# Masked attention scores: VectorE adds the mask inside the maximum for 128 of 384 score units, under a re-searched order

## What is computed

```python
def _attention(v_in, k_in, q_in, mask, Wv, Wk, Wq, Wo, bo):      # L0: "self", then "cross"
    energy = jnp.einsum('nqhd,nkhd->nhqk', q, k)
    energy = jnp.where(mask == 0, jnp.float32(-1e+20), energy)
    attn = jax.nn.softmax(energy / jnp.sqrt(jnp.float32(E)), axis=-1)
    out = jnp.einsum('nhqk,nkhd->nqhd', attn, v).reshape(N, Sq, E)
    return out @ Wo.T + bo
# L1: attention without a mask ("l1")
# L2: one key head, mask |key - query| <= 64 ("l2")
scores = jnp.where(keep[None, None], scores, NEG)
probs = jax.nn.softmax(scores, axis=-1)
# L3: attention without a mask ("l3"), then a feed-forward block
```

## Time and profile before

| | |
|---|---|
| median of 3 runs | 2375.08 us (2370.65 to 2376.75) |
| the profiled execution | 2372.76 us, its span 2370.6 us |
| PE busy | 2256.6 us (95% of the span) |
| PE weight loads busy | 1715.8 us (72%) |
| DVE busy | 1599.6 us (67%) |
| ACT busy | 1297.4 us (55%) |
| POOL busy | 517.9 us (22%) |
| mean granted TensorE clock | 0.984 |

### The profile page before, as it was taken

One profiled execution on the slowest core, in us unless ns is written; L12 is line 12 of the kernel. 1 busy time (PEld: TensorE's weight loads), 2 busy tenths in 40 slices (PEclk: granted clock), 3 DMA queues, 4 the chain that ended last, 5 costly groups with the idle time before them and its releaser, 6 DMA issues.

```text
span 2370.6 us, 50134 instructions
## 1 busy us (share of the span) xinstructions
PE 2256.6 (95%) x18291; PEld 1715.8 (72%) x18291; DVE 1599.6 (67%) x3311; ACT 1297.4 (55%) x2723; POOL 517.9 (22%) x1120
## 2 busy tenths in 40 slices
PE   6999999999998999999999999999999999999966
PEld 4777777777776776877767677877778677777744
DVE  6767687775767677576675767676856767586432
ACT  3554556665464656656464656456465654654522
POOL 4221112231112232121212312111232211122100
PEclk9999999999999999999999999999999999999987
DMA  7322213321212133222122332122231321122100
GB/s 224 114 74 60 60 51 86 105 72 35 77 42 69 33 97 82 63 56 71 40 55 71 100 81 58 48 56 72 67 87 51 83 64 42 51 61 53 48 12 12
DMA packets 164242, 159.17 MB, mean 67 GB/s; under 512 B 17824, under 2 KB 162720, under 8 KB 162976
## 3 DMA queue, kind: packets, MB, share of 16 engines
q1 hardware_dynamic: 164000, 155.97, 24.0%
HBM read 35.71 MB, written 4.19 MB: 17 GB/s over the span
## 4 chain that ended last, share of the span: by engine, by line
PE 68%; issue 18%; DVE 5%; POOL 4%; POOLq 3%; ACT 2%; DVEq 1%; DMA 1%; SPq 0%; ACTq 0%
PE bank L1265 16%; PE bank L1255 12%; PE bank L1294 8%; PE bank L1347 7%; PE bank L1326 6%; PE bank L1290 3%; PE bank L1318 3%; PE bank L1246 3%; PE bank L1466 2%; DVE neg_max L1144 2%; PE bank L1321 1%; PE bank L1314 1%; POOL resid L781 1%; POOL rstd L771 1%; PE bank L1496 1%
## 5 line engine op out<-in xcount | busy, mean ns | idle before, releaser
L1144 DVE TENSOR_REDUCE neg_max<-bank 128x2 f32<-128x512 f32 (+1 forms) x1280 | 762.5, 655 | 217.6 <-PE bank L1294 210.7
L927 ACT ACTIVATE probs<-bank 128x512 f32<-128x512 f32 (+1 forms) x1280 | 645.9, 585 | 325.2 <-PE bank L1326 273.4
L1265 PE MATMUL bank<-par,hidden_t 128*128 128x256 f32 x1792 | 418.9, 384 | 6.3 <-ACT hidden_t L862 3.4
L1265 PEld LDWEIGHTS bank<-par,hidden_t 128*128 128x128 f32 x1792 | 334.1, 191 | 58.8 <-ACT hidden_t L862 9.3
L1326 PE MATMUL bank<-query_stack,key_stack 99*128 99x256 bf16 x2048 | 344.4, 274 | 7.2 <-DMA query_stack<-max_rows 4.0
L1294 PE MATMUL bank<-key_stack,query_stack 96*128 96x256 bf16 x2048 | 326.8, 276 | 16.2 <-issue 13.7
L1255 PE MATMUL bank<-tok_t,par 128*128 128x256 f32 x1408 | 334.6, 387 | 4.4 <-ACT tok_t L862 4.4
L1255 PEld LDWEIGHTS bank<-tok_t,par 128*128 128x128 f32 x1408 | 262.2, 193 | 42.6 <-ACT tok_t L862 7.1
L1294 PEld LDWEIGHTS bank<-key_stack,query_stack 96*128 96x128 bf16 x2048 | 195.9, 99 | 111.1 <-issue 33.4
L1347 PE MATMUL bank<-probs,values 128*17 128x256 f32 x4096 | 256.9, 382 | 1.8 <-DVE neg_max L1144 0.9
L1326 PEld LDWEIGHTS bank<-query_stack,key_stack 99*128 99x128 bf16 x2048 | 194.1, 98 | 62.1 <-issue 12.7
(11 more groups left out here) (167 smaller groups left out, 3271.9 us busy)
## 6 DMA issues: line engine op xcount, KB each, us to landing
query_stack<-query_pieces SPq DMA_DIRECT2D x480, 128.0 KB, 2.4
key_stack<-key_pieces SPq DMA_DIRECT2D x384, 128.0 KB, 2.4
c_in<-in_ctx SPq DMA_DIRECT2D x16, 256.0 KB, 3.3
tok_t<-in_x_features SPq DMA_DIRECT2D x16, 256.0 KB, 2.8
m_in<-in_mask_self SPq DMA_DIRECT2D x16, 256.0 KB, 3.1
x_in<-in_x SPq DMA_DIRECT2D x16, 256.0 KB, 3.1
ctx_t<-in_ctx_features SPq DMA_DIRECT2D x16, 256.0 KB, 3.1
m_in<-in_mask_cross SPq DMA_DIRECT2D x16, 256.0 KB, 3.4
```

What stands on the lines that cost most here:

```text
L927: a_.activation(probs[:, n % PROB_BUFS, k, :, 0:width(l)], bank[:, :, 0:width(l)], ACT.Exp, scale=SCALE[l]).then_inc(exped, 1)
L1144: v.tensor_reduce(neg_max[:, n % HALVES, t, 2 * (u % 4):2 * (u % 4) + 2], bank[:, :, 0:width(l)], AX.X, ALU.max, negate=True).then_inc(max ...
L1265: last = pe.matmul(bank[:, t, :], src[:, t * P:(t + 1) * P], weight, start=(t == 0 and n == 0), stop=(n == len(parts) - 1), skip_group_che ...
```

## The change

A new table `ADDED` names 128 of the masked `max` units (39 `self`, 36 `cross`, 53 `l2`). For these PE writes the bare scores, and DVE does, for each head of each tile, one `tensor_tensor_reduce`: it adds the mask to the scores, negates the sum, writes it back into the bank and keeps the minimum, which is the negated maximum. Each such call is two instructions on DVE, the main one and a short one that reads the accumulator. `PRIMED` shrinks to 98 `max` units (23 `self`, 42 `cross`, 33 `l2`) and 9 `exp` units of `l2`. PE's mask product stays for 158 `max` units (66 `self`, 50 `cross`, 42 `l2`). `ORDER` is another string, 4048 steps in place of 4102, since there are 54 fewer `pre` and `prx` steps.

```diff
+LARGEST = 3.0e38
+ADDED = {
+    ("self", "max"): (
+        "00000000 00000000 00110000 11010000 10010010 11111111 10000000 00000101 "
...
 PRIMED = {
     ("self", "max"): (
-        "00010000 00010010 00001110 01100111 00000001 00000111 00010111 00001111 "
+        "01000011 00001100 00000111 00000001 00000000 00000000 00000011 00011010 "
...
+def added(key):
+
+    b, l, step = key
+    row = ADDED.get((l, step[:3]))
+    return row is not None and row.split()[b][int(step[3:])] == "1" and not primes(b, l, step)
...
+                        if key == FIRST_ADDED.get((b, l)):
+                            if l != "l2":
+                                dve.wait_ge(negs, NEG_NO.upto((b, "self", "inputs" if l == "self" else "negc")))
+                            elif b < SLOTS:
+                                dve.wait_ge(band_ready, 1)
                         for t in range(T):
                             bank = wait_full_unit(dve, key, t)
+                            if added(key):
+                                k = width(l)
+                                for i in range(2):
+                                    h = 2 * (u % 4) + i
+                                    last = v.tensor_tensor_reduce(bank[:, i, 0:k], bank[:, i, 0:k],
+                                                                  neg[l][s][:, t, 0:k], -1.0, LARGEST, ALU.add,
+                                                                  ALU.min, neg_max[:, n % HALVES, t, h:h + 1])
+                                last.then_inc(maxed, 1)
+                                continue
                             v.tensor_reduce(neg_max[:, n % HALVES, t, 2 * (u % 4):2 * (u % 4) + 2], bank[:, :, 0:width(l)],
                                             AX.X, ALU.max, negate=True).then_inc(maxed, 1)
...
-                masked = neg[l][b % SLOTS] if l in neg and primer(key) is None else None
+                fresh = l not in neg or added(key)
+                masked = neg[l][b % SLOTS] if not fresh and primer(key) is None else None
...
-                                         start=l not in neg and i == 0, stop=i == 1, skip_group_check=True)
+                                         start=fresh and i == 0, stop=i == 1, skip_group_check=True)
```

More of the change, by code:

```diff
@@ L129 @@
 PRIMES = (
-    "self.pre2 self.pre1 self.pre3 self.pre4 self.pre6 self.pre5 self.pre7 cross.pre0 cross.pre2 cross.pre1 "
+    "self.pre0 self.pre1 self.pre3 self.pre4 self.pre6 self.pre5 self.pre7 cross.pre0 cross.pre2 cross.pre1 "
     "cross.pre3 cross.pre4 cross.pre5 cross.pre7 cross.pre6 l2.pre0 l2.pre1 l2.pre2 l2.pre3 l2.pre4 l2.pre5 "
-    "l2.pre7 l2.pre6 l2.prx0 l2.prx2 l2.prx3 l2.prx5 "
+    "l2.pre7 l2.pre6 l2.prx0 l2.prx2 l2.prx3 l2.prx4 "
 )
@@ L155 @@
[L155 to L179, removed]
@@ L190 @@
[L190 to L193, removed]
+    "s0RAs0sA0000A000QA0AAAAAAsA1sSAQ00QQ00Q1QB0QAB01B000B02010010ABs1010AsAR1s10R1R0B00B0000S110A0R101A0"
@@ new lines @@
+    "10BR1ss11011011001A2122s10120B0s1B1Ss1s11s0CRQ0B00CQ2010B01B00C110s00012BC120200S10200Q1BBBC00012SB0"
+    "22s11Q0BQ020Q0210Q2010QS01221S1120As2021C20002R2212R022A012R2AR0RA1R1010C1sRD11012021CR0122A12201102"
+    "0110100011111T220C1C1C110110s0C10201S1C1C1022100C1210120102S0CCCC200101201000201B2S20010221021B0BC11"
+    "0102B0222R10B2S2022212211122QCSS221222111222210C11112Q201201E10201111210102100CV11SQ0012R021102012R1"
+    "0210211002121Q0022100012Rs00S1012002201000R0C112122R00A1011RT10R2A10R121A21T0Q1121AQ120Q1BR211001Q22"
@@ new lines @@
+    "11Q02A110212D2202022002B2R2012222Q2100S2RE0010220B20102000210200US220000S0120012201222SSB2D20021S020"
+    "12020BSS12211D210220222222012221201T1S222011TU122DD10011D021031333231121333V33201Q12311132121U331C3C"
+    "131C11CD2303Q2ECUTT11323231323S233U1D33233331DD123DD1E223D22333E123122331E132D244U42424324234D412E22"
+    "24324D424242D4ED4242E2E442U4E3424FT4E4E4E342F3E33T42SE4T4322E44F42FE434VF43T23414FT43244T233T343T3E4"
+    "43343FF324VF2544FU3VU2444434343VS33VFF45UU35353453443U3U3435355454543433334U445435D35544F4U5D35353F5"
@@ new lines @@
+    "4532344543453454554543554534F54DG33D55454D4535553533334553F34435F334F335353F3545335453334545433VE35V"
+    "35V45555E3EE34553EF453354545455354344555554344554435454545544434545343453F444454555TV33V3TVT44453344"
+    "T5TV5435334T3F33VU34U54453445554333344DW534FFT3X34343544DD3D33444U333TW5H445D554T4E44G434E4WT5444455"
+    "E444U454455E543U545454U55345U33455443553545E4455544435533554534445433454G334434454534534434333444V34"
+    "34W4434334433G534343534333343333354455V53V4355VV5V3433V54354534353V753GV5UV36566655G46V5H566565GTU6G"
@@ new lines @@
+    "G56U555V555655GG65565F6GW75G7H6X76775H6HW6775F75F7T64X53WH6FFHU6656767X57U567H76HHX66X6HX5767H6775H7"
+    "GH6656665767657757H677H775HI777557G5777755775557556753X5557X76HX7576H755G6555H75X5577GX77767755756G5"
+    "77776X7577GW6765775775776X7657I67X6H56H777HW56WI566656I8H67688756786686WIY78676686766688IZW677YI6668"
+    "W78Y6768767W8W6886Y6776YYY687758786866767786876778688868G7877887G788G6G88786777J6G77686I8I6677787XJ7"
+    "I88I66I776768667I6867I7678I678I76766I7XI87668886687866I7Y66YH68Y886Y86Y6868Y7668J8788787677868888H7X"
@@ new lines @@
+    "88878868H7YK888Y7X7886XX8H76I6686W778688W786867W8HI8786787I7867W7787768W77877W7X67I787I66877868W66X7"
+    "66787886866866766668676668686787868876h678868W878W7887G6Z8G8X87768g8868X778G6GZ8X78768867G7667767787"
+    "76X86767876767768676677Wg76767787Jg668687766887667Y7687666866Y6Y6Y67Yg86678K8Y688g6Y87Yg7Y6688678666"
+    "6Y9W99J8Z997888989JW898888K89J888I888Z99989I8g8IIZ989868h898JIJa9J99h8JZ9J88J889Y89aJK99999a9J988a98"
+    "98a698898a8878a89Y998aaK9a99888J8988a989a8LKJ88aJa8aJ889a888aLa9aa8a9999a98a8aKZKaha8KaZKa8ha9K9ZZ89"
@@ new lines @@
+    "89Z8Z8KL9bhbK99aZ8bKbbba9La99aaaJLbabbKZha9K9bK9a9Ka99bbbLK999abJ9b9a9a9gLg999b99bbL9abab9bJJg9bb99a"
+    "a9Jb9LMa9a99aaaLag9b8Labigb9bab99bgbbLbabbb9baag9bgba9a9ahb9aaa9aLLbbLaLa9aLaa9ah9aba9L999aab9a9h9a9"
+    "a9bM9bLLbaL9b99aaaa99999a9bbbha9aaLabLbbhbaahb9bKhbbL99babbbba9iabbKMa9bbbZaaKKKababZZb9bbb9abZbh9ba"
+    "ab9Zbbb9abaga9aa9bgb99aa9a9abab99a9bZa99aNab9ab9aNbaaibaaa99aa9b99ba9bb99akJ999b9a99jib9bb99abgba9bb"
+    "bKa9b9ba9gbabZaaab9Jb99bbbbaa9bbbJaabb99bJabab9bhgJaaK9Kaggbb9aLaK9abKiaa999bhLaaabaa9haaaha99a9bhba"
@@ new lines @@
+    "a9Mababah99b9ba999LaZZ9bh9bbbZgab9bba99i9b99b99a99bbgh9ai99bab9bhab9bab9ababaaa99ZbbbZbLbL9b9abaa9g9"
+    "a9hbab9caaMcccaMMbcMccjabcbaabMab9cNccaaaMcabMbaccbaaacacaMbccgcabMbaaabbcacaccbcNag9ccbbbcbbccbcaaa"
+    "NNcccbbcMccbcccMabbNMMbNMcacbcbcOaacaccMNcbbiiOiciacccMOccibdbccNbbbcbcbcibckcNkbbNcibcccbdcddcbcbdc"
+    "bbjchcdccbcdkNccdNbdcdbbcbdedcdejdeecceOehecldeMbOcidekekcdeeOjcbjcMddjcddacedeMdedOdMccddddddcddNcd"
+    "ddceNdcedkdcONceNcdeedeecdecNecdeeceeecPOOdOeOececcceOdOccceedecdeOdicediceOccccPedcdcdddccidcOecddd"
@@ new lines @@
+    "edccPdcOddeccdeddOcededddeiddedckdekediedceekkdekkecdcMkkedceeeddecdeeMcedMcdiccccjijcdddcdjccceeeed"
+    "ijeeeNdMdeMcelecieecdcecdcecdccNdNcdeNiNccceddecdjccejceccedddPcddcdccdejedecedcdccedcdddeecjOcddced"
+    "cOdedcdddcOecdcceleOdOdeeccddcdecccdccedceccedeeicccececeeccdeccdcecdeedecdcedjeeceieedeeccljeeecejd"
+    "ecePddjcecePjdcedkddjcedfdlecdfejeefddfdddePekddflkefdefddjededlddfdeeddeefNdNfcNkeekeddfdeekeefNNdk"
+    "feeffPedPeePdkePeffdejPffdeedffPdPffedfddffePPffkfPfdfdjfldfdddPkfffdPedfffedfdddffldfeldefOffdPddfl"
@@ L194 @@
+    "edfedlfdefddfedffOfdelldOfffdleffOfffdfdfffeffkfffefeeOfkffffeefdeffffedefePPeffefPfdPleedfdeleeeeff"
+    "ffdddfdffdfflefffffPfeeejjfeffeeffeefffeffffeffffffeefffefdfefefefefflePfeflllffefffffffefPlffflefff"
+    "flfflPlfPfffffffffffffffffffffffffffffeffffffffffffffffffffffffffffffffff"
 )
@@ L268 @@
 WORK_NO = Numbers(lambda l, step: step in THROUGH_WORK)
-FIRST_MASKED = {}
+FIRST_MASKED, FIRST_ADDED = {}, {}
 for _key in SCHEDULE:
     if _key[2][:3] == "max" and primer(_key) is None:
-        FIRST_MASKED.setdefault(_key[:2], _key)
+        (FIRST_ADDED if added(_key) else FIRST_MASKED).setdefault(_key[:2], _key)
 PRIME_NO = Numbers(lambda l, step: step[:3] in ("pre", "prx"))
```

37 lines of the change are left out of this document (15 added, 22 removed).

## The result

The changed kernel takes 2340.4 us (median of 4 runs, 2338.95 to 2344.25), the one before 2375.4 us beside it. The ratio is 0.9859, with a 95% interval of 0.9841 to 0.9877: 1.4% faster. By the two medians that is 35.0 us, by the ratio 33.5 us. The forecast was 2345.6 us, 1.2%. The profiled execution took 2344.25 us, where the sum had 2343.3; that these two agree to 1 us is luck, since it was the slowest of the four.

The account below looks back on a forecast made before the run. PE's stream of matmuls was taken as the bound: 2372.76 us less 29.5 us of PE work, plus 0 for hidden DVE work and unchanged waits, gave 2343.3 us, or 2345.6 us for the median; range 2328 to 2374 us.

Parts of the forecast that it names:

- the sum: Whole kernel: profiled 2372.76 us less 29.5 us of PE work plus 0 for waits gives 2343.3 us.
- PE's saving, 29.5 us: Mask products on PE: 88 wide and 68 narrow fewer, 8 narrow back, so 29.5 us less.
- The spacing: Price of a PE mask product from start to start: 0.22 us wide, 0.167 us narrow.
- The records' busy time, 53.8 us: PE's mask products priced by record length, 0.388 and 0.327 us: 53.8 us less; the prediction did not take this.
- VectorE's cost, 26 us, hidden: Added maxima on DVE: 0.10 us more per tile, 256 tiles, 26 us, hidden in DVE's idle time.
- the precedent's 0.35 us per instruction: Earlier DVE instruction over 256 columns in SBUF: main part and reader together take 0.35 us from start to start.
- ScalarE's relief, nothing: Priming copies on ACT: 108 fewer, 55 us less busy time, counted as nothing since ACT was not the bound.
- The waits unchanged: PE's idle time in the middle stretch taken as unchanged at 58 us, without a row for the new waits.
- Rival C: New order makes PE wait more, by as much as was taken off: 2375 us, as before; chance 0.14.
- The waits of the earlier trace, read as PE's: PE's largest waits naming DVE's maxima in the kernel before: 14.7 us, with under 1 us to be added.
- PE's busy time lower by 30 to 50 us: Sign expected in the new profile: PE's busy time falls by about 30 to 50 us.
- upper bound: DVE's added instructions if nothing overlaps: 0.42 us more per tile, in all 107 us, DVE at 73%.

Follow-up runs that it names:

- experiment 1: Changed kernel, new order kept, all 128 added units given back to PE's mask product: 2385.5 us, ratio 1.0063 to the kernel before.
- experiment 5: Changed kernel with DVE's plain reduce in all 128 added units, mask left out of those maxima: 2341.2 us, ratio 0.9858 to the kernel before.
- experiment 6: Changed kernel with one more constant reduce and a drain on DVE ahead of each added tile: 2367.9 us, ratio 0.9992 to the kernel before.
- experiment 7: Changed kernel with the remaining 158 units added too: 2361.0 us, ratio 0.9953 to the kernel before; the same with plain, maskless reduces: 2314.7 us, 0.9747.
- experiment 8: Kernel before, old order, with the 52 units that the change moves from priming to DVE added: ratio 0.9999 to the kernel before.
- experiment 2: Kernel before, with its own order and priming, 76 units that had PE's mask product added on DVE: 2362.2 us, ratio 0.9960; repeat 2357.8 us, 0.9935.

## Why the prediction was right, and where it was not

**PE's saving, 29.5 us: right in size.** 148 mask products were gone, and giving back 256 of them cost 48 us of the 50.7 worked out by the same prices (experiment 1). The spacing was the right price. The records' busy time, 53.8 us for this change, would have overshot the measured 35 us. The Trainium skill, Perfetto Trace Analysis, section Identifying the Most-Contended Engine, gives as its reason that pipelined instructions look smaller in the trace. Here they look larger, 0.388 us on record against 0.22 us from start to start; its advice holds all the same. The 4 to 5 us between the sum and the measured gain have no term in the sum.

**VectorE's cost, 26 us, hidden: the size was off, the hiding right.** It took 42 us of busy time: the precedent's 0.35 us per instruction holds for a main part that follows no reader, but one right behind the reader of another took 0.38 us in a bank, so a wide tile costs 0.16 us more than a reduce and not 0.10. It does not arrive in the changed kernel (experiment 5). The margin was thinner than I thought: with DVE at 73% busy a quarter to a third of a further addition is seen (experiment 6), and with all units added more than half (experiment 7).

**ScalarE's relief, nothing: right**, as far as the old order shows it (experiment 8).

**The waits unchanged: right as a number, wrong as a reason.** PE's idle time in the middle went from 58.4 to 53.2 us. But I had taken it as what happens when one has no row for the new waits, as if PE's saving came through by itself in any order. In the old order 30 us of saving brought 10 to 15 us with DVE's mask and 20 without. The changed kernel has the same PE work as experiment 2 (18143 against 18139 matmuls) and is 18 to 24 us faster: that is the new order's part, more than half of the gain. At the heavier load of experiment 1 the same order was worth, by estimate, 6 us, which the intervals do not tell from nothing. So the order counted for more where PE's work had been cut. The comparison has one gap: the old order with all 128 units added was not run, only its 76 and its 52 units apart (experiments 2 and 8). Rival C had the mechanism, waits that grow when PE gets faster (64.6 us of idle time in the middle in experiment 2, from 58.4), but put it on the new order, where it was the old order that had it. With 0.14 for C and no row for the order, the forecast was in part lucky here.

**The waits of the earlier trace rows, read as PE's: a slip without effect.** They are those of PE's weight loads, which run beside its matmuls. The matmuls themselves waited 4.2 us for maxima in the kernel before, not 14.7 us.

**PE's busy time lower by 30 to 50 us: wrong, it fell by 22.6.** Two things have a part. In the opening PE was busy as long as before for 43 matmuls fewer, at the lower clock; by the estimate above that is 5 of the 7 us that are missing from 29.5. And since records overlap, a wait of up to 0.16 us behind a matmul (0.38 less 0.22) still counts as busy, and some of the idle time that grew may be of this kind. This second reason is argued, not shown by a run. The first cannot be all: in the old order, with the opening at a clock of 1.00 as before, PE's busy time fell by 22 to 28 us for 30 us of products taken off.

What stays open: which waits take the missing 10 us in the old order. They are spread, and no single releaser grew by that much. Also open is what the lower clock in the first 60 us costs; it was 0.72 to 0.80 in every profile of the new order here and 0.86 to 1.00 in those of the old one. That the clock and the time go together is visible in the kernel before alone: of its 27 executions beside experiment 1, the five with a mean granted clock of 0.978 took 2374.5 to 2376.4 us and the three with 0.986 or 0.987 took 2362.3 to 2365.8 us. Only the mean of each is on record, not where in the span the clock was low.

## What to carry to other kernels

Price work taken off a busy TensorE by the distance from start to start, not by the records, and do not count on seeing all of it in an order that was made for another balance: here most of the same choice in the old order gave a third to a half of its saving. When an experiment gives work back, count each engine's instructions against the kernel before, and not only against the changed one, before reading it as the worth of what is left. An engine that is busy for 70% of the span took a small addition for nothing here and refused the next one, so test the slack with dummy work of the size of your upper bound before you rely on it. Moving all of a kind of work is not the limit of moving some of it: 128 units on VectorE gained 1.4%, 286 in the same order only 0.5%.

## What the runs showed of the hardware that was not expected

A `tensor_tensor_reduce` over 256 columns with its input and output in a bank takes 0.35 us until the next can start, as it does with both in SBUF, if the main part follows another instruction or a pause. If it starts together with the accumulator reader of the one ahead, it takes 0.38 us in a bank (188 cases against 57), while in SBUF it stays at 0.35 us (318.17 to 318.52 in the earlier trace rows). A drain ahead brings the first of a pair back to 0.35 us (563.66 to 564.01 in experiment 6). The reader is on record for 139 ns with a bank and for 83 ns with SBUF. Plain reads of a bank cost no more than of SBUF, so a read of the bank alone does not explain it; the cause stays open.
